# Values of a cross-attention block: 120 direct products replaced by a stage of seven block products, and a reordered head-pair turn

## The reference

```python
x = _rmsnorm(hidden_states, ln_weight)          # hidden_states = layernorm(x), (8, 128, 512)
h_q = (x @ w_q.T).reshape(b, lq, H, DH)         # H = 32 heads, DH = 128
h_k = (key_value_states @ w_k.T).reshape(b, lk, H, DH)
h_v = (key_value_states @ w_v.T).reshape(b, lk, H, DH)
score = jnp.einsum('bqhd,bkhd->bhqk', h_q, h_k) + position_bias[None]
score = softmax(where(mask, score, -inf))
attn = jnp.einsum('bhqk,bkhd->bqhd', score, h_v).reshape(b, lq, H * DH)
out = hidden_states + attn @ w_out.T
```

## Time and profile before

| | |
|---|---|
| runs, us | 866.61, 866.15, 866.02 (median 866.15) |
| the profiled execution, us | 864.54 |
| span of its trace, us | 862.8, granted TensorE clock 1.000 |
| TensorE matmul busy | 846.6 us (98%) |
| TensorE weight load | 749.9 us (87%) |
| VectorE | 526.6 us (61%) |
| ScalarE | 370.5 us (43%) |
| GpSimd | 405.4 us (47%) |
| DMA | 38% of 16 engines, 111.84 MB, mean 130 GB/s |

### The profile page before, as it was taken

The page is one execution under the profiler, slowest core; times in us unless marked ns, Lnnn a source line. Parts: engine busy times, 40 slices in busy tenths (PEclk is TensorE's granted clock), DMA queues, the critical chain, the costliest instruction groups (busy, mean ns, idle before and its releaser), DMA issues.

```text
span 862.8 us, 15524 instructions
## 1 busy us (share of the span) xinstructions
PE 846.6 (98%) x5044; PEld 749.9 (87%) x5044; DVE 526.6 (61%) x907; ACT 370.5 (43%) x1040; POOL 405.4 (47%) x374
## 2 busy tenths in 40 slices
PE   8999999998999999999999999999999999999998
PEld 7878888887899989898999989898999989897786
DVE  6885555659474564747374654747373755658862
ACT  5664444444443444434343534434343434453410
POOL 1476666666664536272544536272634546243200
PEclk9999999999999999999999999999999999999999
DMA  9144554455343525243332524242433515342001
GB/s 315 51 151 153 161 189 161 146 183 177 104 166 110 176 73 169 81 151 122 128 130 95 176 73 152 97 152 102 147 112 112 170 60 171 126 142 98 2 25 73
DMA packets 51765, 111.84 MB, mean 130 GB/s; under 512 B 6816, under 2 KB 24224, under 8 KB 49824
## 3 DMA queue, kind: packets, MB, share of 16 engines
q1 hardware_dynamic: 51744, 111.57, 38.2%
...
...
## 4 chain that ended last, share of the span: by engine, by line
PE 88%; DVE 4%; POOL 3%; issue 2%; DMA 1%; ACT 1%; SPq 1%; POOLq 0%; DVEq 0%
PE proj_ps L1331 40%; PE proj_ps L1510 13%; PE proj_ps L1566 11%; PE score_ps L1362 3%; PE score_ps L1396 3%; PE proj_ps L1741 3%; PE pv_ps L1566 2%; PE turn_ps L1566 2%; PE pv_ps L1396 2%; PE turn_ps L1396 2%; PE pv_ps L1362 1%; PE turn_ps L1362 1%; PE proj_ps L1759 1%; DMA acc<-in_x 1%; PE pv_ps L1331 1%
## 5 line engine op out<-in xcount | busy, mean ns | idle before, releaser
L413 POOL TENSOR_TENSOR w_lo<-w_raw,w_hi 128x1024 fp32r<-128x1024 f32 x34 | 81.6, 2405 | 150.6 <-ACT w_hi L567 150.6
L1331 PE MATMUL proj_ps<-w_hi,ct_hi 128*128 128x256 f32 x512 | 146.3, 286 | 0.2 <-DVE w_lo L932 0.2
L1331 PE MATMUL proj_ps<-w_lo,ct_hi 128*128 128x256 f32 x512 | 144.8, 283 | 0.0
L1331 PE MATMUL proj_ps<-w_hi,ct_lo 128*128 128x256 f32 x512 | 144.8, 283 | 0.0
L424 POOL TENSOR_TENSOR comb<-mask_add,bias_sb 128x1024 f32<-128x1024 f32 x32 | 77.3, 2437 | 132.4 <-DVE attn L1095 132.4
L587 ACT ACTIVATE attn<-attn,neg_max 128x128 f32<-128x128 f32 x256 | 99.3, 390 | 49.1 <-DVE neg_max L1084 49.1
L1117 DVE TENSOR_TENSOR acc<-proj_ps,acc 128x512 f32<-128x512 f32 x112 | 77.4, 692 | 67.4 <-PE proj_ps L1331 66.6
L1331 PEld LDWEIGHTS proj_ps<-w_hi,ct_hi 128*128 128x128 f32 x512 | 98.1, 192 | 1.4 <-DVE w_lo L932 0.4
L1331 PEld LDWEIGHTS proj_ps<-w_hi,ct_lo 128*128 128x128 f32 x512 | 98.1, 192 | 0.6
L1331 PEld LDWEIGHTS proj_ps<-w_lo,ct_hi 128*128 128x128 f32 x512 | 98.1, 192 | 0.0
L1331 PE MATMUL proj_ps<-w_hi,tf_hi 128*128 128x512 f32 x240 | 95.3, 397 | 1.4 <-ACT v_sb L572 1.4
...
## 6 DMA issues: line engine op xcount, KB each, us to landing
...
attn<-block_spill SPq DMA_DIRECT2D x120, 128.0 KB, 2.9
qt<-q_spill SPq DMA_DIRECT2D x15, 1024.0 KB, 5.2
...
bias_sb<-in_bias SPq DMA_DIRECT2D x16, 128.0 KB, 4.9
...
```

The lines of the kernel that those rows point to most:

```text
L413: pool.tensor_tensor(lo, w_raw[:, k, :], hi.bitcast(F32), ALU.subtract).then_inc(w_lo_done[k], 1)
L1331: mm = pe.matmul(o, lhs(l, n), rhs(r, n), start=(start and n == 0 and m == 0), stop=(stop and n == terms - 1 and m == 2))
```

## The change

- V of phases 1 to 15 is no longer made inside the turns. A stage between the Q stage and the attention (`v_group`, four groups of 3, 4, 4 and 4 head pairs) makes it with seven block products for each group; a block is half of the group's columns by half of the input width. One block product (`v_product`) is four row tiles of six matmuls with 384 columns (group 0) or 512 (the others). The results, after ScalarE copies (`v_copies`), VectorE sums (`v_add`, `v_21`) and GpSimd sums (`v_last_sums`), are stored to `v_spill` in DRAM. The weights come as an array of their own, `v_weights`, laid out by block; their sums are made in `w_raw` (`v_first_sums`, `v_second_sums`).
- The form tiles turn in a ring of four slots of `w_hi`, `w_lo`. Form 0 of group 0 and its first sums are on VectorE, inside the last Q phase; forms 0 (later groups), 1 and 2 on GpSimd, forms 3 to 6 on VectorE.
- The scores of phase 0 stand before the last block product of group 3, its last sums inside the first softmax (`first_iteration`).
- A turn on TensorE is now `all_scores`, `k_stage`, `out_all`, `values`: the output products of a turn are those of the phase before, and the four `pv` stand together at the end. Three sets of PSUM banks (`out_banks`, `pv_banks`, `score_banks`) replace the old assignment. K of phase 1 also goes through `k_stage`, so the 48 direct matmuls are gone.
- V of a phase is read back by two loads of 512 KB (`load_v`), which the SyncE queue issues between the two block exchanges. The queue's other loads of a turn (bias, Q, output weights, K weights) move ahead of the exchanges.
- In the last turns the scores of phase 15 stand before `pv` of phase 14, and no V product is left between them.

```diff
+VG = 4
+VPAIRS = ((1, 4), (4, 8), (8, 12), (12, 16))
+VN = tuple((hi - lo) * DH for lo, hi in VPAIRS)
+VFORMS, VCOPIES, VPOSTS, VTILES = 7, 12, 16, 4
...
+        out_banks = [proj_ps[3], score_ps[0], score_ps[1], proj_ps[0], proj_ps[1], proj_ps[2], proj_ps[3], score_ps[0]]
+        pv_banks = [score_ps[1], proj_ps[0], proj_ps[1], proj_ps[2]]
+        score_banks = [turn_ps, pv_ps, score_ps[0], score_ps[1]]
+        vx_ps, vy_ps = [score_ps[0], score_ps[1], turn_ps, pv_ps], proj_ps
...
+            for g in range(VG):
+                after_lo(g, 3)
+                load_v_block(g + 1, R12) if g < VG - 1 else load_w(WO, 0)
+                after_lo(g, 4)
+                load_v_block(g + 1, R21) if g < VG - 1 else load_w(WV, NPH)
+                for n in range(2):
+                    sp.wait_ge(v_copied, g * VCOPIES + 10 + 2 * n)
+                    store_v(g, "11", v_11, 0, 0, n)
+                    if n == 0:
+                        after_lo(g, 5)
+                        load_v_block(g + 1, R11) if g < VG - 1 else load_w(WK, 1)
+                if g < VG - 1:
+                    after_lo(g, 6)
+                    load_v_block(g + 1, R22)
+                for n in range(2):
+                    sp.wait_ge(v_post, g * VPOSTS + 4 * n + 4)
+                    store_v(g, "12", v_12, 0, 1, n)
+                if g < VG - 1:
+                    for n in range(2):
+                        sp.wait_ge(v_last, g * VTILES + 2 * n + 2)
+                        store_v(g, "22", v_w, 1, 1, n)
+                for n in range(2):
+                    sp.wait_ge(v_post, g * VPOSTS + 14 + 2 * n)
+                    store_v(g, ("21a", "21b")[n], v_11, 1, 0, n)
+            for n in range(2):
+                sp.wait_ge(v_last, (VG - 1) * VTILES + 2 * n + 2)
+                store_v(VG - 1, "22", v_w, 1, 1, n)
...
+            def load_v(a, t):
+                sp.dma_start(v_sb[:, t * BU:(t + 1) * BU, :], v_spill[:, t * BU:(t + 1) * BU, a * HP * DH:(a + 1) * HP * DH] if isinstance(a, int)
+                             else v_spill[:, t * BU:(t + 1) * BU, bass.ds(a * (HP * DH), HP * DH)]).then_inc(v_in[t], 16)
...
+            sp.wait_ge(v0_stored, 16)
+            for t in range(2):
+                sp.wait_ge(v_stored[("21a", "21b")[t]], 16 * VG)
+                load_v(0, t)
+            load_q(1)
+            refill_k(0)
+            for n in ("11", "12", "22"):
+                sp.wait_ge(v_stored[n], 32 * VG)
+            for t in range(2):
+                exchange(0, t)
+            def turn(a):
+                load_bias(a + 1)
+                load_q(a + 1)
+                refill(WO, a)
+                if not isinstance(a, int):
+                    refill_k(a)
                 for t in range(2):
-                    exchange(p - 1, t)
-                if isinstance(p, int):
-                    sp.wait_ge(kt_done, 3)
-                    sp.wait_ge(kt_hi_done, 1)
-                    sp.wait_ge(kt_lo_done, 1)
-                    load_block(3, k_buf[:, 0:2, :], 1, 0)
-                load_q(p)
-                load_bias(p + 1)
-                sp.wait_ge(k_lo, p * PRODUCTS)
-                load_w(WK, p + 2)
-                refill(WV, p + 2)
-                refill(WO, p + 1)
-            turn(1)
-            with sp.Fori(2, LAST) as p:
-                turn(p)
+                    exchange(a, t)
+                    if t == 0:
+                        for n in range(2):
+                            sp.wait_ge(pv_done, a * UNITS - UNITS + 2 * n + 2)
+                            load_v(a, n)
+            with sp.Fori(1, LAST - 1) as a:
+                turn(a)
...
+            rest_kt(1, 2)
+            rest_kt(2, 3)
+            v_rest(0, 1)
+            rest_kt(3, 4)
+            v_rest(0, 2)
+            v_second_sums(0)
             pool.wait_ge(mask_done, 1)
             add_mask(0)
-            rest(WK, 1)
-            rest(WV, 1)
-            rest(WO, 0)
+            for g in range(1, VG):
+                v_rest(g, 0)
+                v_first_sums(g)
+                v_rest(g, 1)
+                v_last_sums(g - 1)
+                v_rest(g, 2)
+                v_second_sums(g)
+            k_forms(0)
+            v_last_sums(VG - 1)
...
+            lead_k(0)
+            iteration(0)
+            act.wait_ge(v_prod, VG * VFORMS * VTILES)
+            lead(WO, 0)
+            lead(WV, 1)
+            lead_k(1)
+            attention(0)
+            with act.Fori(1, LAST - 1) as a:
+                iteration(a)
+                lead_k(a + 1)
+                act.wait_ge(out_done, a * B)
+                lead(WO, a)
+                attention(a)
...
+                    v_rest(0, 0)
+                    v_first_sums(0)
...
+            def first_iteration():
+                last = VG - 1
+                add_bias(0, 0)
+                add_bias(0, 1)
+                add_bias(0, 2)
+                v_21(last, 0)
+                normalise(0, 0)
+                v_21(last, 1)
+                normalise(0, 1)
+                dve.wait_ge(v_stored["12"], 32 * VG)
+                turn_probs(0, 0)
+                v_21(last, 2)
+                add_bias(0, 3)
+                v_21(last, 3)
+                normalise(0, 2)
+                normalise(0, 3)
+                turn_probs(0, 1)
+                k_posts(0)
...
+            def v_product(g, k, x, banks, start, free):
+                wait_v_lo(pe, g, k)
+                for m in range(VTILES):
+                    free(m)
+                    for c in range(2):
+                        for n, (l, r) in enumerate(((0, 0), (1, 0), (0, 1))):
+                            w = v_form(g, r, k)[:, c * VN[g]:(c + 1) * VN[g]]
+                            mm = pe.matmul(banks[m][:, 0:VN[g]], x[l][:, c, m * P:(m + 1) * P], w, start=(start and c == 0 and n == 0),
+                                           stop=(c == 1 and n == 2), skip_group_check=not start)
+                    mm.then_inc(v_prod, 1)
...
+            def v_group(g):
+                v_product(g, 0, VB["11"], vx_ps, True, posted(g - 1, 13) if g else lambda m: pe.wait_ge(xt_raw_done, B))
+                if g == 0:
+                    pe.wait_ge(kt_lo_done, 1)
+                v_product(g, 1, KT1, vy_ps, True, posted(g - 1, 9) if g else stage_a_left)
+                v_product(g, 2, VB["21"], vx_ps, False, copied(g, 0))
+                v_product(g, 3, VB["22"], vy_ps, False, copied(g, 4))
+                if g == 0:
+                    pe.wait_ge(kt_lo_done, 2)
+                v_product(g, 4, KT2, vx_ps, True, copied(g, 8))
+                if g == 0:
+                    pe.wait_ge(kt_lo_done, 3)
+                v_product(g, 5, KT3, vy_ps, True, posted(g, 2, 2))
+                if g == 0:
+                    pe.wait_ge(kt_lo_done, TF)
+                if g < VG - 1:
+                    v_product(g, 6, KT4, vx_ps, True, posted(g, 1, 2))
+                    return
+                pe.wait_ge(v_post, g * VPOSTS + 8)
+                for u in range(UNITS):
+                    scores(0, u)
+                v_product(g, 6, KT4, vy_ps, True, posted(g, 9))
...
+            k_stage(0)
+            pe.wait_ge(v_post, VG * VPOSTS)
+            values(0)
+            with pe.Fori(1, LAST - 1) as a:
+                all_scores(a)
+                k_stage(a)
+                out_all(a)
+                values(a)
+            all_scores(LAST - 1)
+            k_stage(LAST - 1)
+            out_all(LAST - 1)
+            all_scores(LAST)
+            values(LAST - 1)
             pe.wait_ge(w_lo_done[WO], LAST)
-            out_proj(LAST, 0, True)
+            open_out(0)
```

591 lines of the change are left out of this document (336 added, 255 removed).

## The result

| | before | after |
|---|---|---|
| median, us | 866.09 (864.57 to 866.61, 4 runs) | 887.51 (885.68 to 889.74, 4 runs) |
| the profiled execution, us | 864.54 | 886.86 |
| span, us; granted clock | 862.8; 1.000 | 885.1; 0.985 |

The ratio is 1.0247, 95% interval 1.0230 to 1.0265: slower by 21.4 us, where the prediction says 857.0 and gives "slower" 0.15.

The account below looks back on a forecast made before the run. TensorE, busy 98% of the span, was taken as the bound: -35.9 us of work plus waits of 5.5, 15.5, 2.6 and 3.1 gave -9.2, so 855.3 profiled and a median of 857.0 us; range 847 to 869.

Parts of the forecast that it names:

- slower: Outcome that the changed kernel takes longer than the one before, given chance 0.15.
- TensorE's work: TensorE's matmul balance: 188.9 us removed, 153.0 added, with 384-column matmuls taken at 0.173 us and 512-column ones at 0.227.
- -35.9: TensorE's own balance in us, from fewer and wider products, before the added waits.
- Wait 3: Every loop turn, before `pv` of unit 2: block reads land 0.2 us late, times 13 turns, 2.6 us.
- the first rival: Second exchange, behind 1 MB of V in the queue, sets the turn: 870 us, deciding from 0.9 us per turn; chance 0.15.
- Bounds 0 and 1.5: Limits in us on the wait per loop turn, the upper for V slower by a third or gaps before transfers.
- Wait 2: Phase 0: first `pv` 12.9 us late behind queued stores and loads, second exchange 2.8 more; 15.5 us in the sum.
- phase 0 hardly waits: Rival: stores and loads overlap, only half 1's softmax sets the end, 5 instead of 15.5 us; total 847; chance 0.13.
- Wait 1: V stage: form 0 some 2 us late, second sums late by some 2 and 1.2 in groups 0 and 1; 5.5 us.
- a V stage above 150 us: One of the signs listed in advance as showing the forecast wrong.
- VectorE and GpSimd hold each other up: Rival in the V stage: the two engines contend, 14 instead of 5.5 us; total 865; chance 0.12.
- Wait 4: Last softmax: the first transpose waits for phase 14's lo tiles, 36.8 against TensorE ready at 33.6; 3.1 us.

Follow-up runs that it names:

- e1: Changed kernel with the loop's two V loads moved to the head of SyncE's turn, ahead of bias and Q loads: 865.29 us, ratio 0.9984 to the kernel before.
- e6: Changed kernel with e1's turn and a new SyncE order before the first turn, write 0 early and Q of phase 1 last: 851.29 us, ratio 0.9826.
- e15: Changed kernel with GpSimd's third context lo tile moved behind the second sums of group 0, the mask behind the sums of group 2: 881.35 us, ratio 1.0160.
- e12: Changed kernel with queue, softmax and V-stage reorderings, plus phase 15's second normalisation behind the last two lo tiles of phase 14: 855.81 us, ratio 0.9876.

## Why the prediction was wrong

**TensorE's work, right.** Matmuls of 384 columns start 0.173 us apart (0.173 taken), of 512 0.227, and a turn without a wait is 27.56 us (27.5). The -35.9 stands.

**Wait 3, the step that failed: 0.2 us a turn forecast, 1.7 measured.** Turns 2 to 13 take (384.2 - 32.6) / 12 = 29.3 us against e1's 27.56 (1.5 us of the difference is listed as wait, the rest comes with the restart), turn 1, at half clock in part, 32.6. The mechanism was named, as a term and as the first rival; its size was off. The count put the landing of write 1 at 21.9 us after the first score. It came at 22.25 in the turn shown, and in turns 2 to 13 at 22.1 to 23.25, mean 22.5. The read-back was counted as 4.1 us from the first read's issue to `pv`, and takes 5.0 (472.44 - 467.44; 4.7 to 5.3 in the other turns): the 2.9 us of the earlier trace rows is a median over reads, and `pv` waits for the last of four. These are errors of 0.6 and 0.9 us on average, in a chain that the forecast itself gave no margin: 29.3 - 27.7 = 1.6 us a turn, 19 in twelve turns, and 4.9 in turn 1. The "Bounds 0 and 1.5" were too narrow on the side that mattered, and a chance of 0.15 for the rival was too low for a step with no slack at all. The rival "decides from 0.9 us per turn", and 1.7 is above that. With 1.7 in 13 turns the prediction's own sum would be 857.0 - 2.6 + 22.1 = 876.5; what is still missing to 887.5 lies in turn 1, phase 0 and the V stage.

**The clock, a term that was missing.** Windows of the changed kernel (columns: length, PE, PEld, DVE, ACT, POOL busy, granted clock, DMA share, GB/s):

```profile
373.00:383.00 10.00, 7.35 (x33) 7.08 (x34) 2.07 (x3) 1.79 (x3) 4.91 (x5) 0.50 0.30 98
383.00:385.00 2.00, 2.00 (x11) 2.00 (x11) 0.69 (x1) 0.60 (x1) 0.00 (x0) 0.50 0.00 0
...
412.00:416.00 4.00, 3.80 (x19) 3.83 (x20) 0.69 (x1) 0.78 (x2) 0.01 (x1) 0.57 0.00 0
```

After 14.3 us idle, from 373.6 on, TensorE runs at 1.2 GHz until 385.1, over the second wait of 2.05 us: two `pv` units take 3.6 us instead of 1.8, twice, which makes 3.6 us in phase 0, and the first scores of turn 1 are 1 us longer; the wait of 2.3 at turn 1's end brings half clock once more. The waits of 1.0 to 2.0 us in the later turns of this trace don't. I priced each wait at its length; the long one cost its length and a third more. This price varies between runs: in e1, after 14.7 us idle, the clock was at 0.50 until 378.5, full until 381.9, and at 0.50 again until 385.3, and phase 0 took 41.6 instead of 42.4 us.

**Wait 2, right in place, within 1.5 us.** 14.3 + 2.05 = 16.4 us where 12.9 + 2.8 = 15.7 was counted; what stands in the queue ahead of the exchange sets it, as e6 shows by taking it away. The working had small slips that cancel in part: the items named add up to a write at 26.9 and not 27.5, and 27.5 + 1.31 + 2.9 is 31.7 and not 31.4. Measured, the write had landed at 28.5 and `pv` started at 33.0. Of phase 0's miss of 5.0, 0.9 is wait against the 15.5 in the sum and 3.6 the clock. The rival "phase 0 hardly waits" needs another order than the change has.

**Wait 1, 5.5 forecast, 9.8 measured** (the pure products make 138.0 of 147.8). The three waits that the prediction names came nearly as counted: 1.82 us for form 0 (some 2), 2.45 and 1.55 before the fourth products of groups 0 and 1 (2 and 1.2). What it put at nothing are three small waits, 0.52 + 0.17 + 0.22 us, the half clock behind the fourth product, 1.6, and some 1.5 at the restarts. The half clock is no fixed cost: e1, without it, waits 0.92 and 0.49 us further on instead and takes 147.8 as well. By the prediction's own sign, a V stage above 150 us (with its last product 153.2), this too was wrong. The cause named, second sums late by GpSimd's lo tiles ahead of them, is shown by e15 for group 0, but it is not the whole of that wait: 1.3 us of it is the lo tile of form 3 beside the mask. The rival that VectorE and GpSimd hold each other up (14 us) shows in the lo tiles of group 0 and in none of groups 1 to 3, where VectorE's twelve take 1.22 or 1.23 us each. For form 0, 768 columns took 2.43 us beside GpSimd, and the next operation 0.96 without it. Two rows of VectorE, then GpSimd's:

```profile
192.15 2.43 DVE L1227 TENSOR_TENSOR w_lo<-w_raw,w_hi 128x768 fp32r<-128x768 f32 x1
194.68 0.96 DVE L1233 TENSOR_TENSOR w_raw<-w_raw 128x768 f32<-128x768 f32 x1
...
189.03 4.73 POOL L604 TENSOR_TENSOR xt_lo<-comb,xt_hi 128x1024 fp32r<-128x1024 f32 x2 [4.44 <-ACT xt_hi L839]
```

The Trainium skill (SBUF — State Buffer, Who interferes with whom) says that a VectorE instruction with two SBUF inputs contends with a GpSimd instruction that reads SBUF, for ports that are an exclusive lock. The trace agrees: GpSimd's pair ran until 193.76, and VectorE's instruction ended 0.82 us after that.

**Wait 4, right.** 2.9 us for the lo tiles (3.1 forecast), and the stretch takes 45.6 where 46.4 was counted; e12 shows that one normalisation is 1.0 of it.
